# Attention block on one core: values ahead of scores on TensorE, three pairs behind, with three buffers for the exponentials

## What is computed

```python
xn = _layernorm(x)
# attention
x1 = _rmsnorm(xn, norm_w)
q, k, v = split(x1 @ Wq), split(k_of(x1 @ Wkv)), split(v_of(x1 @ Wkv))
q, k = _head_rmsnorm(q, q_gamma), _head_rmsnorm(k, k_gamma)
sim = einsum('bhid,bhjd->bhij', q, k)
sim = tanh(sim / 50.0) * 50.0 * 64 ** -0.5
attn = softmax(sim)
out = merge(einsum('bhij,bhjd->bhid', attn, v)) @ Wo
# feed-forward, with products of some token rows added to the weights
h = gelu(xn @ (W1 + scale * m1).T + b1)
ffn = h @ (W2 + scale * m2).T + b2
return x + out + ffn
```

## Time and profile before

| what | value |
|---|---|
| median of 3 runs | 1063.51 us (1062.15 to 1065.46) |
| the profiled execution's own time | 1067.33 us |
| its span, first to last instruction | 1065.1 us |
| mean granted TensorE clock | 0.994 |
| busy: TensorE matmul, weight loads | 97%, 79% |
| busy: VectorE, ScalarE, GpSimd | 88%, 92%, 92% |
| low parts on GpSimd (L1073) | 256 of 1.90 us, 485.1 us |
| tanh and exponentials (L654, L661) | 512, 538.2 us |
| values on TensorE (L557 to L559) | 6144 matmuls |

### The profile page before, as it was taken

How to read it: one execution, slowest core, us unless ns; L and a number is a source line. 1 busy time by engine, 2 the same in 40 slices (tenths; PEclk the granted TensorE clock), 3 DMA queues, 4 the chain that set the end, 5 groups by cost and what they waited for, 6 DMA issues and landing times.

```text
span 1065.1 us, 34270 instructions
## 1 busy us (share of the span) xinstructions
PE 1034.3 (97%) x12905; PEld 845.9 (79%) x12905; DVE 937.7 (88%) x2218; ACT 976.0 (92%) x1417; POOL 980.2 (92%) x912
## 2 busy tenths in 40 slices
PE   7689999999999999999999999999999999999997
PEld 6468888788888888888888888888888888888876
DVE  6998999988999988999998999998989998899972
ACT  4599999999999999999999999999999999999995
POOL 6799999999999999999999999999989999999883
PEclk8899999999999999999999999999999999999999
DMA  3354444444445435444444444444454444544351
GB/s 117 56 82 83 81 82 81 73 82 90 77 82 82 77 79 89 77 88 76 79 80 86 78 88 79 76 81 83 81 84 80 72 80 87 82 85 79 71 92 31
DMA packets 310491, 85.44 MB, mean 80 GB/s; under 512 B 282020, under 2 KB 309816, under 8 KB 310328
## 3 DMA queue, kind: packets, MB, share of 16 engines
q1 hardware_dynamic: 310328, 83.25, 43.6%
HBM read 11.09 MB, written 4.19 MB: 14 GB/s over the span
## 4 chain that ended last, share of the span: by engine, by line
PE 44%; POOL 26%; issue 10%; DVE 9%; ACT 5%; SPq 4%; DMA 2%; POOLq 0%; DVEq 0%; ACTq 0%
POOL probs_lo L1073 10%; PE ps_scores L531 9%; PE ps_y L568 5%; PE ps_aux L506 5%; POOL sq_k L1054 5%; POOL halves L1065 4%; PE ps_aux L517 4%; PE ps_o L557 4%; PE ps_aux L446 3%; PE ps_y L567 3%; PE ps_o L559 3%; PE ps_o L558 3%; POOL rstd L984 2%; DVE halves L835 2%; PE ps_aux L447 2%
## 5 line engine op out<-in xcount | busy, mean ns | idle before, releaser
L1073 POOL TENSOR_TENSOR probs_lo<-probs 128x1024 f16<-128x1024 f32 x256 | 485.1, 1895 | 20.6 <-ACT probs L661 19.5
L654 ACT ACTIVATE clamped<-ps_scores 128x1024 f32<-128x1024 f32 x256 | 265.4, 1037 | 43.4 <-PE ps_scores L531 36.3
L661 ACT ACTIVATE probs<-clamped 128x1024 f32<-128x1024 f32 x256 | 272.8, 1066 | 2.6
L557 PEld LDWEIGHTS ps_o<-v_hi,probs 128*128 128x128 bf16 x2048 | 183.7, 98 | 56.6 <-issue 53.5
L531 PE MATMUL ps_scores<-heads_T 64*128 64x256 f16 x3072 | 212.1, 271 | 5.0 <-ACT clamped L654 3.1
L557 PE MATMUL ps_o<-v_hi,probs 128*128 128x65 bf16 x2048 | 214.2, 195 | 2.7 <-DVE ps_n L826 1.1
L558 PE MATMUL ps_o<-v_lo,probs 128*128 128x64 bf16 x2048 | 211.8, 193 | 0.0
L559 PE MATMUL ps_o<-v_hi,probs_lo 128*128 128x65 bf16 x2048 | 211.3, 193 | 0.0
L446 PE MATMUL ps_aux<-w_hi,xhT_hi 128*128 128x512 f32 x384 | 175.3, 456 | 15.0 <-DVE qk L876 10.7
L558 PEld LDWEIGHTS ps_o<-v_lo,probs 128*128 128x128 bf16 x2048 | 187.5, 99 | 0.0
L559 PEld LDWEIGHTS ps_o<-v_hi,probs_lo 128*128 128x128 f16 x2048 | 187.4, 97 | 0.0
(11 more groups left out here) (96 smaller groups left out, 2009.7 us busy)
## 6 DMA issues: line engine op xcount, KB each, us to landing
heads_T<-halves SPq DMA_TRANSPOSE x512, 2.5
x_in<-in_L_attn_tokens_dram SPq DMA_DIRECT2D x32, 128.0 KB, 2.4
x_res<-in_L_attn_tokens_dram SPq DMA_DIRECT2D x32, 128.0 KB, 2.3
out_dram<-y_sb SPq DMA_DIRECT2D x32, 128.0 KB, 2.0
sel_raw<-xn SPq DMA_DIRECT2D x192, 4.0 KB
qk<-in_L_attn_Wkv_dram SPq DMA_DIRECT2D x2, 512.0 KB, 5.3
qk<-in_L_attn_Wq_dram SPq DMA_DIRECT2D x1, 512.0 KB, 3.5
qk<-in_L_ffn_W_dram SPq DMA_DIRECT2D x2, 256.0 KB
```

The source lines that it names most:

```text
L557: pe.matmul(full, hi[:, col], v_hi[:, par, u, h], start=(u == 0), stop=False)
L654: nc.scalar.activation(clamped[:].rearrange("p j n -> p (j n)"), ps_scores[:].rearrange("p j n -> p (j n)"), ACT.Tanh).then_inc(clamp_done, 1)
L661: nc.scalar.activation(probs[:, pair % RING].rearrange("p j n -> p (j n)"), clamped[:].rearrange("p j n -> p (j n)"), ACT.Exp, bias=LIFT, ...
L1073: g.tensor_tensor(probs_lo[:, buf].rearrange("p j n -> p (j n)"), probs[:, buf].rearrange("p j n -> p (j n)"), probs[:, buf].rearrange("p ...
```

## The change

On TensorE the values of a slot now come ahead of its scores, and they are those of the pair three slots back (`VALUES_LAG = 3`), so the pairs 5, 6 and 7 of a batch fall into slots 0, 1 and 2 of the next step. VectorE's divisions follow the same number. `probs` and `probs_lo` have three buffers (`RING = 3`), chosen by the running number of the pair over all batches. The transposes oT 3 move from slot 2 to slot 3, and so the four y steps of slot 2 stand together. The tail has one block of values more. The tables of the other three engines are the same.

```diff
-    [("scores",), ("values",), ("oT", 2, -1), ("low", 1, 0), ("y", 2), ("oT", 3, -1), ("y", 2)],
-    [("scores",), ("values",), ("hid", 0, 0), ("hid", 1, 0), ("y", 3)],
...
+    [("values",), ("scores",), ("oT", 2, -1), ("low", 1, 0), ("y", 4)],
+    [("values",), ("scores",), ("oT", 3, -1), ("hid", 0, 0), ("hid", 1, 0), ("y", 3)],
...
-RING = 2
-VALUES_LAG = 2
+RING = 3
+VALUES_LAG = 3
...
@@ values, exp and lo_part
-                buf = pair % RING
+                buf = (PAIRS * b + pair) % RING
...
@@ last_batch
+                values(st, 0, -1, PAIRS - 3)
                 turn(0)
                 turn(1)
-                values(st, 0, -1, PAIRS - 2)
-                turn(2)
+                values(st, 1, -1, PAIRS - 2)
                 wait(pe, gelu_done, 4 * b + 4)
                 wait(pe, y_added, b)
                 pe.wait_ge(half_lo_made, PAIRS * batches)
                 products(0, HC)
+                values(st, 2, -1, PAIRS - 1)
+                turn(2)
                 pe.wait_ge(oT_copied, 4 * b + 2)
                 products(HC, HC + 4)
-                values(st, 1, -1, PAIRS - 1)
+                turn(3)
                 pe.wait_ge(oT_copied, 4 * b + 3)
                 products(HC + 4, HC + 6)
-                turn(3)
                 pe.wait_ge(oT_copied, 4 * b + 4)
```

More of the change, by code:

```diff
@@ L51 @@
 TENSOR_STEPS = [
[3 rows of a table removed]
-    [("scores",), ("values",), ("hid", 0, 0), ("hid", 1, 0), ("y", 3)],
[4 rows of a table removed]
+    [("values",), ("scores",), ("k", 2, 1), ("k", 3, 1), ("oT", 0, -1)],
+    [("values",), ("scores",), ("xT", 0, 2), ("low", 0, 0), ("y", 2), ("oT", 1, -1), ("y", 2)],
+    [("values",), ("scores",), ("oT", 2, -1), ("low", 1, 0), ("y", 4)],
+    [("values",), ("scores",), ("oT", 3, -1), ("hid", 0, 0), ("hid", 1, 0), ("y", 3)],
[4 rows of a table added]
 ]
@@ L660, in exp @@
                 wait(act, attended, PAIRS * b + pair + 1 - RING)
-                nc.scalar.activation(probs[:, pair % RING].rearrange("p j n -> p (j n)"),
+                nc.scalar.activation(probs[:, (PAIRS * b + pair) % RING].rearrange("p j n -> p (j n)"),
                                      clamped[:].rearrange("p j n -> p (j n)"), ACT.Exp, bias=LIFT,
```

## The result

The changed kernel takes 1135.54 us (median of 4 runs, 1134.11 to 1138.02) against 1064.49 us (4 runs, 1062.15 to 1066.87) for the kernel before on the same chip. The ratio is 1.067, 95% interval 1.0638 to 1.0702: slower by 71 us. The forecast was 1110 us with a range up to 1128, so the direction was right and the time lies 7.5 us above the range.

A forecast was written before the change was run, and what follows sets the result against it. A closed chain across four engines was taken to set the batch, 31.76 us, growing to 33.35: 1.59 more over 29 steps, 46 us, on a median of 1063.51, gives 1110 us; range 1074 to 1128.

The forecast's parts named there:

- What bounds the kernel: One closed chain per batch through TensorE, ScalarE, GpSimd and VectorE, from slot 0's k3 product to the next: 31.76 us.
- Order inside a slot, the boundary from values to scores: TensorE, values followed by scores: a gap of 0.10 us, bounds 0 and 0.21; a slot then costs TensorE what it did.
- Slot 1: TensorE after slot 0's k3 product: values of slot 1 start at 1.24 us, its scores at 2.07 instead of 1.34.
- New wait 1: TensorE, transposes oT1 wait for ScalarE's copy oT0, made behind the later tanh: 0.61 us.
- new wait 2: TensorE in slot 2, the third y step waits for ScalarE's copy oT1, made behind tanh: 0.61 us.
- Slots 3 and 4: Slot 3's scores to tanh 0.90 us, next tanh 5.21 later, low part 3.98 later; Newton steps still in time for slot 4's values.
- To slot 7: Product v3 in slot 6 loses 0.32 us to the k0 copy; slot 7's scores at 27.79, next k3 product at 33.35.
- Steps 30 and 31 and the tail, nothing: Only steps 1 to 29 counted; the tail's extra values block (0.73 us) fills an existing 0.82 wait: no cost.
- The third buffer, nothing: Third buffer of exponentials: removes at most 2.6 + 3.1 us of waits, off the chain, so no gain.
- Slower by less: Rival: ScalarE's copies come in time, only values ahead of slot 3's scores count; 1072 or 1094 us; chance 0.30 (1067 to 1098).
- Faster: Rival: earlier values let VectorE divide earlier and release GpSimd's scaling and low part; 24.6 us less, 1039; chance 0.07.
- No change: Rival: removed waits were nothing, and no gap between values and scores returns 0.30, cancelling 0.29; 1063.5 us; chance 0.06.

The follow-up runs named there:

- the last run: Kernel before (scores first, lag 2, two buffers) with transposes oT3 moved to slot 3 and ScalarE's copy oT3 behind the exponential: 1056.01 us against 1064.25, ratio 0.9929.

## Why the direction was right and the size was not

**What bounds the kernel: right.** A swap on the chain (slot 1) moves the time by 35 us where one off it (slots 5 and 6) moves it by nothing. And the period follows S3, as a closed chain must. Read from one batch of each trace:

| kernel | S3 after k3 | period |
|---|---|---|
| changed | 10.68 | 34.08 |
| copies ahead of the tanh | 10.02 | 33.41 |
| scores first in slot 1 | 9.62 | 33.02 |
| that, with the second copy ahead of the tanh | 9.34 | 32.73 |

**Order inside a slot, the boundary from values to scores: right.** It was bounded by 0 and 0.21 and taken as 0.10. V to S is 0.81 in slot 1, 0.82 in slot 2 and 0.83 in slot 3 (528.76 to the scores at 529.59), for 0.83 forecast: a boundary of 0.08 to 0.10.

**Slot 1, "Now V1 is at 1.34 - 0.10 = 1.24": the step that failed.** It took TensorE's own place as V1's start and looked at who waits for the copy, not at what V1 itself waits for. The description of the kernel lists `qk_normed` among its conditions. V1 stands at 1.84 and S1 at 2.65, 0.60 and 0.58 later than forecast. The trace of before already had the number: there too the normalise of slot 0 began at 522.42 and took 0.69, ending 1.70 after k3 (521.41). Hidden behind the scores, which kept V1 until 2.10 (523.51), it cost nothing; with the values first it stands bare. VectorE's and TensorE's timelines of before:

```profile
522.42 0.69 DVE L826 TENSOR_TENSOR ps_n<-qk,ps_o 128x512 f32<-128x512 f32 x1
```

```profile
523.51 0.20 PE L557 MATMUL ps_o<-v_hi,probs 128*128 128x65 bf16 x1
```

**New wait 1 and new wait 2: right.** The waits are shown as 0.37 each, at the oT1 products and the third y step, with the restart on top. S1 to S2 is 4.21 (forecast 6.29 - 2.07 = 4.22) and S2 to S3 3.82 (forecast 3.78).

**Slots 3 and 4: right.** S3 to tanh is 0.89 (forecast 0.90), tanh to tanh 5.21, to the low part 3.98, S3 to S4 4.47 (forecast 4.50), all near the forecast. The Newton steps were in time: no wait of V4 shows.

**To slot 7: nearly.** S4 to S7 is 13.23 for 13.22, with v3 held for the k0 copy as forecast. From S7 to k3 0.13 was missing: VectorE's halves of slot 0 waits for ScalarE's half, which comes behind the late tanh. The steps there had been put one behind the other on VectorE alone.

The two together, 0.60 + 0.13 = 0.73, are the whole difference between 34.08 and 33.35. Over 29 batches they are 21 us: 1110 + 21 = 1131, and 1.0 of the 4.5 us left is the kernel before, at 1064.49 here where the sum started from 1063.51.

**Steps 30 and 31 and the tail, nothing: too small.** The sum counted 29 batches. But the last scores stand 54.9 us after the last k3 where they stood 49.6, since these steps have slots 1 to 3 too, and only 1.0 comes back in the tail behind them (15.0 us for 16.0). That is 4.3 us that the sum had put at nothing. Against it stand the 3.0 us of longer batches in the kernel before. Those 3.0 us are of one execution, and what is left, about 2 us, lies within the 4.7 us over which the four executions of the kernel before are spread.

**The third buffer, nothing: right as the change stands** and with the scores first (1062.24, and the last run). It was incomplete in one respect. With the values first and the lag of 2, a wait for the low part appears (22.5 us), and the longer lag takes the wait away.

**The rivals.** "Slower by less" fell with the two copy waits. "Faster" fell as argued: the exponential never waited for its ring. "No change" fell with the same two waits, and with a boundary of 0.08 to 0.10 where it wanted none. The range had room for one unknown boundary and one small wait of 0.2; it had none for a whole dependency overlooked, three times that size.

## What to carry to other kernels

When a block of instructions is moved ahead in an in-order stream, go through every semaphore that this block waits for, at its new time; a wait that the trace doesn't show may have been covered by the work it has just overtaken. When two engines hand work to each other in a ring, price the move by the closed chain's period, from start to start, and not by how busy an engine is. And try each part of a change alone: here the order lost 71 us, the longer lag and its buffer brought nothing without it, and a side effect of the rearrangement, one transpose moved to another slot, is the part that gains some 8 us once its copy is placed to match.

## What was not expected of the hardware

VectorE's normalise, a product of 128 x 512 fp32, took 686 ns in the mean with one operand in SBUF and one in PSUM, beside a GpSimd at work for 86% of the time. With both operands in SBUF it took 1256 ns. Single ones took more; this is the timeline of VectorE in that run:

```profile
554.01 2.01 DVE L828 TENSOR_TENSOR ps_n<-qk,rnorm_sb 128x512 f32<-128x512 f32 x1
```

Beside it, the timeline of GpSimd in the same run:

```profile
553.57 1.88 POOL L1075 TENSOR_TENSOR probs_lo<-probs 128x1024 f16<-128x1024 f32 x1
```

The low part had started first and ends at 555.45, and the normalise ends 0.56 us behind it. The whole run is so: 126 of the 256 normalises start while a low part, a square or a scaling of GpSimd runs, and each of them ends 0.55 to 0.56 us behind the end of a GpSimd instruction. The shortest takes 0.69 us. The reverse is there too: a low part that starts within a normalise (at 534.53) takes 2.23 us, where the mean of the changed kernel's is 1.89.

GpSimd's own instructions grew too: squares from 1040 to 1254 ns, its scaling from 1047 to 1156 ns in the mean. The Trainium skill, SBUF — State Buffer, section SBUF: two separate sides, says that VectorE with two SBUF inputs and GpSimd lock each other out for whole instructions. The two runs agree with it, with GpSimd reading SBUF in both. No run here varied GpSimd's own operands.
